# A post-norm block with routed experts: the groups' side work in a new order on four engines

## What is computed

```
q, k  = rope(x @ Wq.T), rope(x @ Wk.T)
o     = sum over keys of where(causal, exp(q.k / 16), 0)        # one number per token
x1    = layernorm(x + relu(o @ fc1_w.T + fc1_b) @ fc2_w.T + fc2_b)
xa    = x1 @ P_w.T
C1, C2, C3 = softmax over the top 3 of xa @ U1.T, xa @ U2.T, xa @ U3.T   # 4096 x 12 each
h     = gelu(sum_e C1[:, e] * (x1 @ W1[e].T))
y     = sum_e C2[:, e] * (h @ W2[e].T) + C3 @ b2
out   = layernorm(x1 + y)
```

## Time and profile before

| | |
|---|---|
| three runs | 323.3, 323.63, 323.86 us (median 323.63) |
| the profiled execution: time, span | 323.53 us, 321.8 us |
| TensorE matmul busy | 282.4 us (88%) |
| VectorE busy | 250.2 us (78%) |
| ScalarE busy | 155.8 us (48%) |
| GpSimd busy | 115.0 us (36%) |
| mean granted TensorE clock | 0.981 |
| DMA, mean over the span | 64 GB/s |

### The profile page before, as it was taken

The page is one execution under the profiler, slowest core; times in us unless marked ns, Lnnn a source line. Parts: engine busy times, 40 slices in busy tenths (PEclk is TensorE's granted clock), DMA queues, the critical chain, the costliest instruction groups (busy, mean ns, idle before and its releaser), DMA issues.

```text
span 321.8 us, 6235 instructions
## 1 busy us (share of the span) xinstructions
PE 282.4 (88%) x1976; PEld 191.8 (60%) x1978; DVE 250.2 (78%) x744; ACT 155.8 (48%) x327; POOL 115.0 (36%) x264
## 2 busy tenths in 40 slices
PE   0999999979784989999999999999999997989981
PEld 0444455444333668677677667677678576667770
DVE  0169789999976579689789879888978977887672
ACT  1138747657561381435635634633733753724331
POOL 1000028999999102142332331522333324132221
PEclk9999999999985999999999999999999999999998
DMA  8999999900000000000010001000100010011011
GB/s 232 415 404 229 200 151 211 144 3 0 0 1 0 3 2 0 18 18 18 18 33 17 18 18 29 22 18 18 34 20 16 18 34 19 18 33 26 26 35 37
DMA packets 19235, 20.58 MB, mean 64 GB/s; under 512 B 1600, under 2 KB 18432, under 8 KB 18688
## 3 DMA queue, kind: packets, MB, share of 16 engines
q1 hardware_dynamic: 18480, 19.22, 24.8%
q10 hardware_dynamic: 720, 0.93, 1.0%
HBM read 15.94 MB, written 4.19 MB: 63 GB/s over the span
## 4 chain that ended last, share of the span: by engine, by line
DVE 25%; PE 21%; issue 6%; ACT 5%; POOL 3%; DVEq 0%; POOLq 0%
PE bank L832 17%; DVE early L1202 11%; DVE st L1239 3%; DVE stats L1038 2%; DVE top L1059 2%; ACT x L548 2%; DVE early L1244 2%; PE bank L784 2%; ACT early L657 1%; POOL rstd L391 1%; PE bank L741 1%; DVE mv L1240 1%; ACT x1T L555 1%; ACT early L604 1%; DVE esum L1104 1%
## 5 line engine op out<-in xcount | busy, mean ns | idle before, releaser
L832 PE MATMUL bank<-W,early 128*128 (+1 forms) x630 | 75.5, 273 | 4.4 <-DVE early L1244 2.3
L832 PE MATMUL bank<-W,x1T 128*128 (+1 forms) x630 | 76.9, 277 | 0.5 <-DVE early L1202 0.3
L832 PEld LDWEIGHTS bank<-W,x1T 128*128 128x128 f16 x630 | 60.3, 99 | 19.8 <-DVE early L1202 9.5
L688 PE MATMUL bank<-early,wqk 128*128 128x512 f32 x128 | 64.3, 634 | 8.5 <-DMA gatew<-in_gate 8.5
L1202 DVE SCALAR_TENSOR_TENSOR early<-bank,Csel,early 128x256 f32<-128x256 f32 x124 | 59.3, 479 | 15.0 <-PE bank L832 10.5
L832 PEld LDWEIGHTS bank<-W,early 128*128 128x128 f16 x630 | 60.1, 98 | 14.8 <-DVE early L1244 3.3
L457 POOL TENSOR_SCALAR ve<-mv 128x1 f32<-128x1 f32 x32 | 7.3, 230 | 117.2 <-DVE mv L1240 117.2
L688 PEld LDWEIGHTS bank<-early,wqk 128*128 128x128 f32 x128 | 23.5, 201 | 30.1 <-issue 20.9
L604 ACT ACTIVATE early<-early 128x256 f32<-128x256 f32 x32 | 13.3, 417 | 48.0 <-DVE early L1202 47.9
L499 ACT ACTIVATE qk<-bank 128x512 bf16<-128x512 f32 x32 | 19.0, 594 | 35.6 <-PE bank L688 35.4
L599 ACT ACTIVATE early<-bank,Csel 128x256 f32<-128x256 f32 x31 | 14.6, 472 | 31.0 <-PE bank L832 30.7
(11 more groups left out here) (107 smaller groups left out, 422.3 us busy)
## 6 DMA issues: line engine op xcount, KB each, us to landing
early<-in_xT SPq DMA_DIRECT2D x16, 256.0 KB, 9.8
xs<-in_x SPq DMA_DIRECT2D x32, 128.0 KB, 7.3
out<-early SPq DMA_DIRECT2D x32, 128.0 KB
W<-in_w1T SPq DMA_DIRECT2D x1, 2048.0 KB, 12.0
W<-in_w2T SPq DMA_DIRECT2D x1, 2048.0 KB, 12.3
W<-in_w1T SPq DMA_DIRECT2D x1, 1024.0 KB, 7.6
W<-in_w2T SPq DMA_DIRECT2D x1, 1024.0 KB, 13.8
wqk<-in_wqkT ACTq DMA_DIRECT2D x1, 512.0 KB, 3.8
```

The costliest lines, as they stand in the source:

```text
L688: mm = pe.matmul(bank[PROJ[n % 2]][:, :], wqk[:, k, g, :], xTb[:, c % 4, k, :, :].rearrange("p s n -> p (s n)"), start=(k == 0), stop=(k = ...
L832: mm = pe.matmul(where[:, 0:DIM], lhs(hx, c), w, start=(k == 0), stop=(k == 5))
```

## The change

Every `aux` gets new places for its pieces, and the waits that guard the shared banks now count what TensorE has itself begun (`begun`) instead of being written as formulas of the group number.

- TensorE: `C3_transpose` goes from (0, 0) of its own group to (3, 1) of the group before; both `fc` halves stand in iteration 3; `bias` is at (0, 0) and (2, 0), `route_logits` at (0, 0), the two `x1_transpose` at (0, 1) and (2, 1).
- VectorE, ScalarE and GpSimd follow: the router's steps are one iteration part earlier, both `fc_add` and `norm_stats` are in iteration 3, `norm_scale` is behind `select_of`, all four normalizations are at (0, 0), and `C3T_copy` and one `x1_high` stand at `pos` 0 of iterations 3 and 2.
- The start: `C3_transpose(0)`, `fc(2, 0)` (out of the chunks) and `fc(2, 1)` go between the products of tile 0, with their `fc_add` and `norm_stats(2)` between VectorE's sums; `bias(0, 0)`, the logits of group 1 and `x1_transpose(2, 0)` stand behind tile 0's mixture. On ScalarE `C3T_copy(0)`, the normalizations of group 2 and its `x1_high` come behind the last gate's relu and ahead of tile 0's gelu.

The core of the diff, in the order GpSimd, ScalarE, TensorE, VectorE:

```diff
             def aux(k, s, pos):
-                if (s, pos) == (1, 1) and group(k + 2):
-                    norm_scale(k + 2)
-                if (s, pos) == (2, 1) and group(k + 1):
-                    chosen_exps(k + 1)
-                if (s, pos) == (3, 1) and group(k + 1):
-                    weights_of(k + 1)
-                    select_of(k + 1)
+                if (s, pos) == (1, 0):
+                    if routed(k + 1):
+                        chosen_exps(k + 1)
+                if (s, pos) == (2, 0):
+                    if routed(k + 1):
+                        weights_of(k + 1)
+                if (s, pos) == (3, 1):
+                    if routed(k + 1):
+                        select_of(k + 1)
+                    if later(k + 3):
+                        norm_scale(k + 3)
 
...
                 if (s, pos) == (0, 0):
+                    if later(k + 2):
+                        normed(k + 2, 0)
+                        normed(k + 2, 1)
+                if (s, pos) == (0, 1):
+                    if later(k + 2):
+                        x1_high(k + 2, 0)
+                if (s, pos) == (1, 0):
+                    if routed(k + 1):
+                        exp_route(k + 1)
+                if (s, pos) == (2, 0):
+                    if later(k + 2):
+                        x1_high(k + 2, 1)
+                if (s, pos) == (3, 0):
                     if group(k + 1):
-                        x1_high(k + 1, 1)
-                    if group(k):
-                        C3T_copy(k)
-                if (s, pos) == (1, 0) and group(k + 1):
-                    exp_route(k + 1)
-                if (s, pos) == (2, 0) and group(k + 2):
-                    normed(k + 2, 0)
-                if (s, pos) == (2, 1) and group(k + 2):
-                    normed(k + 2, 1)
-                if (s, pos) == (3, 0) and group(k + 2):
-                    x1_high(k + 2, 0)
+                        C3T_copy(k + 1)
 
...
 
-            aux(0, 0, 0)
-            aux(0, 0, 1)
+            x1_high(1, 1)
             begin(0)
             exps(NCH - 1, 0)
             exps(NCH - 1, 1)
             gate_relu(NCH - 1)
+            C3T_copy(0)
+            aux(0, 0, 0)
+            aux(0, 0, 1)
             gelu(0)
...
+
+            begun = {"fc": 0, "bias": 0, "x1T": 0, "C3T": 0, "logits": 0, "count": 0}
+
             def fc(g, h):
                 T = GT * g // 8
                 if g == 0 and h == 0:
                     pe.wait_ge(ld_rows, 16 * 5)
                 if h == 0:
                     pe.wait_ge(hgT_copied, 2 * (T + 1))
-                    wait(pe, bias_added, 2 * (g - 2))
-                wait(pe, fc_added, 2 * g + h)
+                wait(pe, bias_added, begun["bias"])
+                wait(pe, fc_added, begun["fc"])
+                begun["fc"] += 1
                 for t in (2 * h, 2 * h + 1):
...
                     pe.wait_ge(scale_done, 1)
-                wait(pe, C3T_copied, g)
+                wait(pe, C3T_copied, begun["C3T"])
+                wait(pe, ids_done, begun["count"])
+                wait(pe, dz_done, begun["logits"])
+                begun["logits"] += 1
                 for t in range(GT):
...
                 pe.wait_ge(mask_done, g + 1)
+                wait(pe, C3T_copied, begun["C3T"])
+                wait(pe, dz_done, begun["logits"])
+                begun["count"] += 1
                 tiles = range(1 if g == 0 else 0, GT)
...
                 pe.wait_ge(C3_done, g + 1)
-                pe.wait_ge(ids_done, g + 1)
+                wait(pe, ids_done, begun["count"])
+                wait(pe, dz_done, begun["logits"])
+                begun["C3T"] += 1
                 pe.transpose(bank[MISC][:, 0:P], C3[:, :, :].rearrange("p t n -> p (t n)"), identf[:, :])\
                     .then_inc(C3T_done, 1)
 
             def bias(g, h):
                 pe.wait_ge(C3T_copied, g + 1)
-                if h == 0:
-                    wait(pe, fc_added, 2 * min(g + 3, NG))
-                    wait(pe, bias_added, 2 * g)
-                else:
-                    wait(pe, fc_added, 2 * min(g + 3, NG))
-                    wait(pe, bias_added, 2 * g + 1)
+                wait(pe, fc_added, begun["fc"])
+                wait(pe, bias_added, begun["bias"])
+                begun["bias"] += 1
                 rows = slice(2 * PAD * h, 2 * PAD * (h + 1))
...
                     x1_transpose(k + 2, 0)
-                if (s, pos) == (3, 0) and group(k + 3):
+                if (s, pos) == (3, 0) and k < -1:
                     fc(k + 3, 0)
 
             def aux(k, s, pos):
-                if (s, pos) == (0, 0) and group(k):
-                    C3_transpose(k)
+                if (s, pos) == (0, 0):
+                    if group(k):
+                        bias(k, 0)
+                    if routed(k + 1):
+                        route_logits(k + 1)
                 if (s, pos) == (0, 1):
-                    if group(k + 1):
-                        route_logits(k + 1)
-                    if group(k + 2):
-                        fc(k + 2, 1)
-                if (s, pos) == (1, 1) and group(k):
-                    bias(k, 0)
-                if (s, pos) == (2, 1):
+                    if later(k + 2):
+                        x1_transpose(k + 2, 0)
+                if (s, pos) == (2, 0):
                     if group(k):
                         bias(k, 1)
-                    if group(k + 2):
-                        x1_transpose(k + 2, 0)
-                if (s, pos) == (3, 0) and group(k + 1):
-                    route_count(k + 1)
+                if (s, pos) == (2, 1):
+                    if later(k + 2):
+                        x1_transpose(k + 2, 1)
+                if (s, pos) == (3, 0):
+                    if routed(k + 1):
+                        route_count(k + 1)
+                    if later(k + 3):
+                        fc(k + 3, 0)
                 if (s, pos) == (3, 1):
-                    if group(k + 2):
-                        x1_transpose(k + 2, 1)
-                    if group(k + 3):
-                        fc(k + 3, 0)
+                    if group(k + 1):
+                        C3_transpose(k + 1)
+                    if later(k + 3):
+                        fc(k + 3, 1)
 
...
             route_count(0)
-            aux(0, 0, 0)
             pe.wait_ge(qk_copied, 4 * NCH)
             pe.wait_ge(w_split, NE - NB)
             pe.wait_ge(wlo_done, NB)
             first(range(0, 4))
+            fc(2, 0)
             scores(NCH - 1, 0)
             first(range(4, 7))
+            C3_transpose(0)
+            fc(2, 1)
             scores(NCH - 1, 1)
             first(range(7, NE))
             gate_transpose(NCH - 1)
+            aux(0, 0, 0)
             aux(0, 0, 1)
...
                 if (s, pos) == (0, 0):
-                    if group(k + 2):
-                        fc_add(k + 2, 0)
-                    if group(k + 1):
-                        x1_low(k + 1, 1)
-                if (s, pos) == (0, 1) and group(k + 1):
-                    route_max(k + 1)
+                    if routed(k + 1):
+                        route_max(k + 1)
+                if (s, pos) == (0, 1):
+                    if routed(k + 1):
+                        route_strike(k + 1)
                 if (s, pos) == (1, 0):
-                    if group(k + 2):
-                        fc_add(k + 2, 1)
-                    if group(k + 1):
-                        route_strike(k + 1, 0)
-                if (s, pos) == (1, 1) and group(k + 2):
-                    norm_stats(k + 2)
-                if (s, pos) == (2, 0):
+                    if routed(k + 1):
+                        route_mask(k + 1)
                     if group(k):
                         bias_add(k, 0)
-                    if group(k + 1):
-                        route_strike(k + 1, 1)
-                if (s, pos) == (2, 1) and group(k + 1):
-                    route_mask(k + 1)
-                if (s, pos) == (3, 0):
+                if (s, pos) == (1, 1):
+                    if later(k + 2):
+                        x1_low(k + 2, 0)
+                if (s, pos) == (2, 0):
+                    if routed(k + 1):
+                        route_sums(k + 1)
                     if group(k):
                         bias_add(k, 1)
-                    if group(k + 2):
-                        x1_low(k + 2, 0)
-                if (s, pos) == (3, 1) and group(k + 1):
-                    route_ids(k + 1)
-                    route_sums(k + 1)
+                if (s, pos) == (3, 0):
+                    if routed(k + 1):
+                        route_ids(k + 1)
+                    if later(k + 3):
+                        fc_add(k + 3, 0)
+                    if later(k + 2):
+                        x1_low(k + 2, 1)
+                if (s, pos) == (3, 1):
+                    if later(k + 3):
+                        fc_add(k + 3, 1)
+                        norm_stats(k + 3)
 
...
-
```

(58 more changed lines are left out.)

## The result

The changed kernel takes 315.38 us in the median of four runs (313.49 to 318.2) against 323.75 for the kernel before, a ratio of 0.9722 with an interval of 0.9662 to 0.9783. The run of 318.2 us, a slow one 1.5% above the fastest, is not in the ratio; the other three have a median of 314.34. The forecast was 314.3. The profiled execution took 316.43 us, 7.1 less than the profiled one of before. Its granted clock was 0.968, while the two quicker runs, 313.49 and 314.34 us, had 0.979.

The account below looks back on a forecast made before the run. TensorE was taken as the bound, VectorE close behind, losing 1.9 us per full group to waits. Start +1.65, full groups -6.5, group 5 -2.7, group 6 -1.65 make -9.2: 323.53 to 314.3 us, range 309.5 to 319.

Parts of the forecast that it names:

- Full groups: Groups 1 to 4: early waits vanish, each group goes from 25.58 to 23.95 us, four save 6.5 us.
- The 23.7 us for TensorE's own pieces: Sum of TensorE's mixtures, transposes, logits, fc, bias and count in a full group, without waits: 23.7 of 25.58 us.
- The norm chain: From fc over VectorE statistics, GpSimd power and normalizations to the x1 transpose: 0.25 us late per group; rival 1 us, chance 0.12.
- VectorE's reserve: In a full group VectorE needs 22.8 us, 0.9 less than TensorE.
- Groups 5 and 6: Less side work there, the same waits gone: group 5 saves 2.7 us, group 6 saves 1.65.
- The start: Work put ahead in tile 0 delays its second mixture to 124.8; net cost +1.65 us, bounds 0 to +3.5.
- the rest of group 0: After tile 0's second mixture, waits vanish as in a full group: about 1.5 of 1.9 us.
- the clock falls at the start: Rival: gaps in the new start cost one more slow stretch, about 2 us, total 316.3; chance 0.14.
- the end of the gate transposes: In the start, TensorE finishes the gate transposes at 115.4 us, 1.45 later than before.
- ScalarE's serial list: C3T copy, normalizations, x1 high, gelu, exponentials: with VectorE's tail, 9.35 us from gate transposes to tile 0's second mixture, before 6.15.
- the bank waits: Among tile 0's products, VectorE's added work between sums holds a bank back for some 1.5 us.
- VectorE's pieces: Two fc adds and norm_stats (1.73 us) amid tile 0's sums; start's cost bound 0 if hidden in the half clock.

Follow-up runs that it names:

- run 8: Kernel with the old start and the change's new groups, plus a second unread GpSimd power operation inside norm_scale of groups 3 to 7: 314.81 us.
- run 10: Kernel with the old start and the change's new groups, norm_stats of groups 3 to 7 reading 64 of 256 columns: 308.78 us.
- run 9: Old start with early products and unread matmuls, new groups; the ids' register loads moved from behind the first x1 transposes to behind the logits: 306.48 us.
- run 7: Kernel with the old start and the change's new groups, plus four unread VectorE statistics inside norm_stats of groups 3 to 7: 317.1 us.
- run 2: Changed kernel with 15 unread matmuls in TensorE's first wait, between the third and fourth product of tile 0: 312.44 us.
- run 5: Kernel with the old start and the change's new groups, plus 24 unread matmuls ahead of C3_transpose(0): 309.57 us.
- run 3: Changed kernel with tile 0's gelu ahead of group 2's normalizations on ScalarE and group 1's exponentials later: 315.37 us.
- run 4: Changed kernel with norm_stats(2) behind tile 0's last sum instead of its seventh: 316.4 us.
- run 11: Changed kernel with both 15 unread matmuls in TensorE's first wait and ScalarE's gelu ahead of group 2's normalizations, exponentials later: 312.42 us.

## Why the prediction came out

**Full groups** (forecast 23.95, saving 6.5): 23.65, saving 7.8. All the waits that were named went. Three terms were off. The 23.7 us for TensorE's own pieces was some 0.6 too large: group 2 took 23.67 with 0.14 + 0.39 of waiting, so 23.1 of pieces. Three of the four pairs of the gelu's transposes took 0.22 us from start to start and not 0.36, the logits 0.62 and not 0.70, the C3 transpose 0.21 and not 0.33. The distances had been taken from the old order, where they were longer. The norm chain is 0.14 late and not 0.25, and that it is tight was right (runs 8 and 10). And 0.4 us of hole behind the first x1 transposes was not in the forecast: about half is a wait for VectorE's sum (run 10), the rest the ids' register loads (run 9), which in the old order stood behind an fc pair without a hole (168.16, 169.22 in the earlier trace rows). So -0.6 - 0.1 + 0.4 = -0.3: the errors partly cancel.

**VectorE's reserve** (forecast 0.9 us): too large. By the forecast's own measure, the period less VectorE's waits, it needs 23.67 - 0.4 = 23.3 us and not 22.8, no less than TensorE's 23.1. No run tests its load by itself: runs 7 and 10 changed `norm_stats`, which is part of the norm chain, and what they show (1.27 of 1.4 us added, 0.36 of 0.8 taken away) is seen at the x1 transposes and the mixture behind them.

**Groups 5 and 6** (2.7 and 1.65): 3.1 and 2.0, off the same way as the full groups (the sums started from the same 23.7).

**The start** (forecast +1.65): +5.8. The second mixture of tile 0 came 7.4 us later, with 1.54 us of work done ahead, and the rest of group 0 netted nothing, as its waits went and its first matmuls ran at half clock. That is the rival "the clock falls at the start", in this execution at twice its price. By stages the miss of 4.2 us is 2.7 up to the end of the gate transposes (118.1 against 115.4), nothing in ScalarE's serial list, and 1.5 in the rest of group 0.

Run 2 prices the clock in the changed start at 4.2 + 1.65 = 5.9 us and run 5 in the old one at 1.4; the difference, 4.5, leaves 5.8 - 4.5 = 1.3 us for everything that the forecast's sum had in it (1.65). The chunks of this execution also ended 0.7 us sooner than those of before (the count at 94.18 against 94.87), which was luck and not the change: in runs 2 to 4, with the same chunks, it stands at 94.85 to 95.20. Without that it is 2.0 against 1.65. So the parts of that sum (ScalarE's serial list, the bank waits, VectorE's pieces) were sized well, and the step that failed is giving the clock a chance of 0.14 and one stretch of 2 us. These prices are of one profiled execution with a clock of 0.968; two others had 0.979 and took 313.49 and 314.34 us, at or under the forecast.

The Trainium skill, "TensorE: Matmul & The Clock Gate", section "Why this matters for your kernels", warns of long idle gaps between bursts of matmuls. The wait of 3.47 us agrees, but in run 3 the clock fell at 122 us among gaps of 1.26, 1.16 and 0.89 us, and in run 2 gaps of 1.27, 1.16 and 1.64 us left it at full speed; there the measurement decides.

A table load cost what the profile said: it starts as the gelu ends (123.53 + 0.42, then 123.96) and lasts 1.28 us, and the exponentials start 1.29 us after the load's start. The drain of some 1.38 us that the Trainium skill, "ScalarE: Activation LUTs", section "What ACT_TABLE_LOAD costs", adds to a switch is seen on neither side of it.

That the total agreed with the forecast is in part luck: an error of 4.2 us one way met 2.0 us the other way (1.3 + 0.4 + 0.3), leaving 2.1 in the profiled execution. The mechanism of the groups was right, and that of the start was the forecast's own rival.

Left open: how much room VectorE's load has by itself; and what makes one execution of the same kernel lose the clock for longer than another (runs of one kernel differ by up to 4.7 us, with the granted clock). Exchanging ScalarE's list in a start whose clock is kept was not seen: in the profiled execution of run 11 the clock fell too.

## What to carry to other kernels

Lay out the work of a repeated stage against measured durations of all engines, and look for what is served one piece too late; here that was worth 13 us of 324, with no matmul or vector operation removed. Judge the stage before it separately: work put ahead of a dense stage can cost more in the clock than it saves, if it splits TensorE's work by waits. Matmuls that nobody reads, put in a wait that can't be removed, gave 1.0 us in the old start and 1.9 to 2.9 in the new one. When nothing waits any more, price the slack with an added operation before counting on it, and put the addition outside the chain if an engine's load is what you want to price.

## What the runs showed that was not expected

Unread matmuls in a gap of 3.5 us took the mean granted clock from 0.968 to 0.989 and the profiled time from 316.43 to 311.62 us, while waits of 1.27, 1.16 and 1.64 us behind them stayed as they were and no longer cost the clock. Register loads of six expert ids on TensorE's queue, behind only 0.49 us of matmuls, cost 0.3 us per group more than behind the logits (period 23.6 against 23.33), and 0.33 us stay there.
